# Hybrid megakernel, attention scores: minus the row maximum written into the score banks by ACT and DVE, in place of a fourth matmul

## What is computed

```python
latent_kv = x @ w_kv_down                      # (2, 2048, 128)
k, v = split(latent_kv @ w_kv_up)              # 16 heads of 64
q = (x @ w_q)                                  # 16 heads of 64
att = einsum('bqhd,bkhd->bhqk', q, k) * 64 ** -0.5
att = where(causal, att, -inf)
att = softmax(att, axis=-1)
y = einsum('bhqk,bkhd->bqhd', att, v)
x = x + y.reshape(B, T, 1024) @ w_out
```

## Time and profile before

| | us |
|---|---|
| median of 3 runs | 2118.15 (2118.07 to 2118.34) |
| span of the profiled execution | 2113.7 |
| the rest, outside the span | 4.45 |
| PE busy | 1984.7 (94%) |
| POOL busy | 1425.9 (67%) |
| DVE busy | 1337.2 (63%) |
| ACT busy | 1097.9 (52%) |

### The profile page before, as it was taken

One profiled execution on the slowest core, in us unless ns is written; L12 is line 12 of the kernel. 1 busy time (PEld: TensorE's weight loads), 2 busy tenths in 40 slices (PEclk: granted clock), 3 DMA queues, 4 the chain that ended last, 5 costly groups with the idle time before them and its releaser, 6 DMA issues.

```text
span 2113.7 us, 35206 instructions
## 1 busy us (share of the span) xinstructions
PE 1984.7 (94%) x12886; PEld 1240.9 (59%) x12886; DVE 1337.2 (63%) x2728; ACT 1097.9 (52%) x2236; POOL 1425.9 (67%) x812
## 2 busy tenths in 40 slices
PE   8997788999999999999989999999999999999898
PEld 6775454555655555555555655555555555555466
DVE  7786555576656666666665657576756575656443
ACT  5775543455545454545455444545445445444585
POOL 1333225778687878787857687868786878687822
PEclk9998899999999999999999999999999999999999
DMA  3000000000000000000000000000000000000001
GB/s 124 1 1 1 0 7 13 13 19 10 13 18 16 13 19 12 19 10 19 13 12 17 12 20 11 17 12 20 11 18 11 20 11 18 11 14 11 26 26 60
DMA packets 29243, 37.01 MB, mean 18 GB/s; under 512 B 6928, under 2 KB 20368, under 8 KB 29072
## 3 DMA queue, kind: packets, MB, share of 16 engines
q1 hardware_dynamic: 29072, 34.76, 5.4%
HBM read 30.02 MB, written 4.46 MB: 16 GB/s over the span
## 4 chain that ended last, share of the span: by engine, by line
PE 63%; DVE 14%; POOL 12%; ACT 6%; issue 4%; DMA 1%; POOLq 0%; ACTq 0%; SPq 0%; DVEq 0%
PE heads_out L918 16%; POOL acc L1416 10%; PE beside L723 9%; PE scores L723 7%; PE two_heads L874 7%; PE scores L897 4%; PE scores L903 4%; PE scores L899 4%; PE scores L901 4%; DVE part_max L1112 3%; ACT prob L1331 2%; PE two_heads L723 2%; PE beside L929 2%; PE heads_out L723 1%; DVE wQK_lo L1073 1%
## 5 line engine op out<-in xcount | busy, mean ns | idle before, releaser
L1416 POOL TENSOR_TENSOR acc<-acc,prob 128x1024 f32<-128x1024 f32 (+3 forms) x512 | 1017.9, 1988 | 195.4 <-ACT prob L1331 140.1
L1331 ACT ACTIVATE prob<-scores 128x512 f32<-128x512 f32 (+3 forms) x1280 | 579.4, 539 | 649.2 <-PE scores L903 289.0
L1112 DVE TENSOR_REDUCE part_max<-two_heads 128x2 f32<-128x1024 f32 x384 | 469.3, 1222 | 280.5 <-PE two_heads L874 279.7
L918 PE MATMUL heads_out<-prob,V 128*64 128x512 f32 (+3 forms) x2560 | 544.4, 547 | 0.0
L1109 DVE CUSTOM_DVE_ANT_0 two_heads<-two_heads,mask 128x128 f32<-128x128 f32 (+3 forms) x512 | 242.0, 514 | 180.4 <-PE two_heads L874 180.4
L874 PE MATMUL two_heads<-k_hi,q_hi 64*128 64x512 f32 (+3 forms) x1280 | 274.1, 424 | 62.8 <-DVE part_max L1112 30.6
L918 PEld LDWEIGHTS heads_out<-prob,V 128*64 128x64 f32 x2560 | 156.7, 137 | 232.4 <-issue 209.6
L874 PEld LDWEIGHTS two_heads<-k_hi,q_hi 64*128 64x128 f32 x1280 | 120.6, 184 | 256.6 <-issue 133.4
L897 PE MATMUL scores<-q_hi,k_hi 64*128 64x512 f32 (+3 forms) x1280 | 236.1, 364 | 0.8 <-DVE k_lo L1100 0.5
L903 PE MATMUL scores<-neg_max,sel 64*128 64x512 f32 (+3 forms) x1280 | 235.6, 362 | 0.0
L901 PE MATMUL scores<-q_lo,k_hi 64*128 64x512 f32 (+3 forms) x1280 | 235.5, 362 | 0.0
(11 more groups left out here) (301 smaller groups left out, 2898.7 us busy)
## 6 DMA issues: line engine op xcount, KB each, us to landing
rden<-rden_rows SPq DMA_DIRECT2D x128, 128.0 KB, 2.9
X<-u SPq DMA_DIRECT2D x8, 512.0 KB, 8.7
out<-X SPq DMA_DIRECT2D x8, 512.0 KB, 2.9
wQK_raw<-wQuery SPq DMA_DIRECT2D x16, 192.0 KB, 3.1
wO_raw<-wOut SPq DMA_DIRECT2D x16, 128.0 KB, 2.8
wV_raw<-wValue SPq DMA_DIRECT2D x8, 128.0 KB, 2.9
den<-den_rows SPq DMA_DIRECT2D x64, 4.0 KB
rden_rows<-den SPq DMA_DIRECT2D x64, 4.0 KB, 1.3
```

The source lines that it names most:

```text
L918: made = pe.matmul(heads_out[head(h), x0:], V[vn % NVS][:, tt, p % 2, head(h)], prob[step % NPROB][:, h, x0:], start=t == 0, stop=t == TPB ...
L1112: made = ve.reduce_max(part_max[:, t, :, c:c + 1], two_heads[:, :, 0:width], AX.X)
L1331: ac.activation(prob[step % NPROB][:, h, x0:], bank(task, h)[:, x0:], ACT.Exp).then_inc(empty(task, h)[0], 1)
L1416: po.tensor_tensor(total[:, :, x0:], total[:, :, x0:], new[:, :, x0:], ALU.add).then_inc(acc_ok, 1)
```

## The change

- The fourth pass L903, the tiles `sel` and `neg_max`, the transposes L882 and the copies L1316 are gone.
- `row_max`, 128 queries by 8 values, goes to a DRAM row `top_rows` (1024 fp32, heads first) by a DMA of single elements from SP, and comes back from there in one DMA, broadcast to all 128 partitions, into `top` (128 x 2 x 512 fp32, 512 KB; two buffers). The task is called `spread_max`.
- A new task `seed` stands in the list for each step, one iteration ahead of its scores. ACT writes -`top` into the score banks (576 instructions: 384 of 1024 columns for both heads together, and 64 each of 768, 512 and 256 columns in the diagonal steps). On the 128 columns of the diagonal, DVE writes min(-`top`, `limit`) instead (256 instructions of 128 x 256, the `scalar_tensor_tensor` below); `limit` is +3e38 where the key is allowed and -3e38 where it isn't.
- The three passes start with `start=False` and accumulate on the seed. The mask of L1122 after the scores is gone, and ACT takes the exponential of both heads in one instruction (640 in place of 1280).
- Where the bank last held another kind of product, PE first runs two plain matmuls over it (`opened`), which happens at the start of the attention only.

```diff
@@ Plan.attention
+            if self.layers_done:
+                for step in steps[s + 2:s + 4]:
+                    self.need("seed", *step)
+            while spreads and spreads[0][0] <= s and self.unseeded(spreads[0][1] - NMAX):
+                self.need("spread_max", spreads.pop(0)[1])
             for idx, t in steps[max(0, s - 2):s]:
                 self.need("weigh", idx, t)
                 self.need("accumulate", idx, t)
@@ tensor_program, score
-                    for h in range(2):
-                        pe.matmul(bank(task, h)[:, x0:], sel[head(h), :], neg_max[idx % NMAX][head(h), x0:], start=False, stop=True).then_inc(full(task, h)[0], 1)
+                    if c == j:
+                        w.wait_ge(seeded_masked, plan.seeds[idx, t][0]["DVE"])
+                    else:
+                        w.wait_ge(seeded, plan.seeds[idx, t][0]["ACT"])
...
+                    for n, (k, q) in enumerate(terms((k_hi[g], k_lo[g]), (q_hi[i], q_lo[i]))):
+                        for h in range(2):
+                            made = pe.matmul(scores[:, first + h, x0:], k[head(h), kc], q[head(h), x0:], start=False, stop=n == 2, skip_group_check=True)
+                    made.then_inc(full(task)[0], 1)
@@ vector_program
-                        for h in range(2):
-                            w.wait_ge(*full(task, h))
-                        ve.tensor_tensor(scores[:, first:first + 2, x0:x0 + P], scores[:, first:first + 2, x0:x0 + P],
-                                         limit[:, :].unsqueeze(1).broadcast_to([P, 2, P]), ALU.min).then_inc(masked, 1)
+                        w.wait_ge(*top_here(idx))
+                        if x0 < BLK - P:
+                            w.wait_ge(seeded, plan.seeds[idx, t][0]["ACT"])
...
+                        ve.scalar_tensor_tensor(out=scores[:, first:first + 2, x0:x0 + P], in0=top[idx % NMAX][:, :, x0:x0 + P], scalar=-1.0,
+                                                in1=limit[:, :].unsqueeze(1).broadcast_to([P, 2, P]), op0=ALU.mult, op1=ALU.min).then_inc(seeded_masked, 1)
@@ scalar_program
+                        ac.activation(scores[:, first:first + 2, x0:], top[idx % NMAX][:, :, x0:], ACT.Copy, scale=-1.0).then_inc(seeded, 1)
...
-                    for h in range(2):
-                        w.wait_ge(*full(task, h))
-                        ac.activation(prob[step % NPROB][:, h, x0:], bank(task, h)[:, x0:], ACT.Exp).then_inc(empty(task, h)[0], 1)
+                    w.wait_ge(*full(task))
+                    ac.activation(prob[step % NPROB][:, :, x0:], scores[:, first:first + 2, x0:], ACT.Exp).then_inc(empty(task)[0], 1)
@@ sync_program
+                elif kind == "minus_max":
+                    idx = task[1]
+                    w.wait_ge(row_max_ok, idx + 1)
...
+                    sp.dma_start(top_rows[idx % NTOP, :].rearrange("(a p) -> p a", p=P), row_max[:, idx % 2, :, :].rearrange("p h t -> p (h t)"), allow_slow_non_contiguous=True).then_inc(top_out[idx % 2], 16)
+                elif kind == "spread_max":
+                    idx = task[1]
+                    w.wait_ge(top_out[idx % 2], 16 * (idx // 2 + 1))
...
+                    sp.dma_start(top[idx % NMAX].rearrange("p h x -> p (h x)"), top_rows[idx % NTOP:idx % NTOP + 1, :].broadcast_to([P, 2 * BLK])).then_inc(top_in[idx % 2], 16)
```

202 lines of the change are left out of this document (113 added, 89 removed).

## The result

The changed kernel takes 2451.85 us (2445.93 to 2463.09, 4 runs), the kernel before 2118.24 in the same session: a ratio of 1.1581 (95% interval 1.155 to 1.1612), 334 us slower. Slower was forecast, but by 3%; the time lies 167 us above the upper end of the range.

What follows compares the result with a forecast made beforehand. PE was taken as the main bound, with 63% of the last-ending chain plus 4% issue. 2113.7 - 112 + 177 = 2179 us of span, plus 4.45 outside it, gave 2183 us, slower by 3%; range 2025 to 2285 us.

Steps and rivals of the forecast that it cites:

- -112 + 177: Whole span: PE's saved passes and transposes, then DVE's held seeds, work queued behind them and bank 0, both at 67%.
- PE's gain: On PE: 129 us from passes and 38 from transposes, 167 less in all, counted as -112 us.
- the factor: On PE's savings and new delays: 67%, PE's share of the last-ending chain with issue, taken to move the end.
- 32 us of bank 0: Full iterations whose filler used bank 0: ACT's seed waits 0.4 us in each of some 80.
- the walk: One iteration followed from its first score pass: ACT's full-step seed hidden by PE's fillers and `weigh`, unless bank 0 was used.
- the place: Where full steps end and a diagonal begins: PE took 6.47 us for the iteration, with two fillers.
- My own ring: ACT in a full iteration: exponentials end by 3.05 us, first seed at 4.1 plus 0.6 for each filler ahead.
- 168 + 64 us: Diagonal iterations: 128 holds of DVE's second seed at 1.3 us, plus 0.5 us each for the reduction queued behind.
- the first seed's hold: DVE's first seed of a diagonal pair, held by POOL: taken as hidden by PE's own work.
- with the holds at half price: The forecast's own lower bound, with holds of DVE's seeds costing half: 2115 us.
- ten iterations ahead: Row maxima were said to lie some ten iterations ahead of their use, so scatter and broadcast count as hidden.
- Rival C: Units with j = 1 start some 7 us late, as scatter and broadcast take 16 us: 2295 us, chance 0.06.

Runs made afterwards that it cites:

- e4: The kernel before without the fourth pass L903, the making of neg_max kept, maximum not subtracted: 2059.5 us.
- e7: e3 with ACT's seeds cut to 64 columns a head, PE's first pass beginning the sum anew: 2076.8 us.
- e3: The changed kernel with both contiguous rows to DRAM and DVE taking the minimum in the bank: 2219.5 us.
- e2: The changed kernel with the scatter written as 128 contiguous rows of 32 bytes instead of single elements: 2404.6 us.
- e11: e2 with POOL's accumulates (t > 1) cut to 64 columns a head, DVE's seed unchanged: 2184.0 us.
- e10: e7 with DVE's seed from two SBUF tiles put back in place of the minimum in the bank: 2275.2 us.
- e1: The changed kernel with ACT seeding all columns and DVE taking the minimum in the bank, single-element scatter kept: 2376.7 us.
- e13: e3 with constant seeds and no broadcast, but the single-element scatter, SP's wait for it and a small read to a spare tile: 2252.6 us.
- e9: The kernel before with both heads' exponentials merged into one instruction: 2110.5 us, ratio 0.9989.

## Why the prediction was wrong, step by step

From before to the changed kernel one path leads through the runs (ratio differences, in us): pass gone, -55 (e4); all the rest of the change with short ACT seeds and contiguous rows, the transposes gone too, +19 (e7); full length of ACT's seeds, +141 (e3); the hold, +185 (e2); single elements, +44 (the changed kernel). The sum is +334, as it must be for differences of neighbours. On another path the last two are 157 and 72.

The forecast was -112 + 177 = +65, so 269 us are missing. Along this path they are 76 on PE's gain (-36 measured for the first two parts, in place of -112), 120 on ACT's seeds (141 in place of 21), 30 on the hold (185 in place of 155) and 44 on the DMAs (in place of nothing).

**PE's loss: direction right, size too large.** Forecast -112 for passes and transposes, of which 86 are the passes; e4 shows 55 for these, with an interval of 16. The failed step is the factor: 67%, PE's share of the chain with the issue time, was applied to all of it, and it was 0.43 (0.3 to 0.55). With 129 us gone, PE waited longer for the reductions and ACT for the mask (above). PE still has 62% of e4's chain, so the share doesn't tell this; why the factor is lower was not tried further. The transposes, 25 us of the forecast, were not tried alone. PE's busy time, which was to fall by 160 us, rose by 62.

**ACT's seeds: the largest miss.** Forecast: hidden, but for 32 us of bank 0, 21 after the factor; measured: 141 for their length alone. The price of one was right, 1.04 against 1.02 us measured. (ScalarE: Activation LUTs in the Trainium skill, section What ACT_TABLE_LOAD costs, gives 1039 ns by its formula; the trace agrees, with 1020 for the median.) What failed was the walk: it was made at one place, where PE took 6.47 us for an iteration. 320 iterations between 290 and 2030 us take 5.4 us in the mean, and 5.0 with the two passes of 0.23 gone; the place had more of PE's work than most. My own ring had the first seed at 4.1 us plus 0.6 for each filler, the second one 1 us later. At 5.0 us there is no cover for two of them. That this is what failed is argued from the ring; what e7 shows is the price of the length. I also wrote nothing for what stands behind the seeds on ACT: `oT_hi`, for which POOL waited 291.3 us in the changed kernel, 207.2 in e3, 116.5 in e7, 107.1 before.

**DVE's seed: mechanism right, size near, in part by luck.** Forecast 168 + 64 us, times 0.67: 155. Measured 185 and 199 without the scatter, 72 beside it. That POOL's instruction holds it is shown (e11), and the ends 0.29 and 0.30 us behind POOL's ends are those of the earlier trace rows (0.28). (SBUF — State Buffer in the Trainium skill, section Who interferes with whom, has the rule of the shared ports; e2 and e11 agree: a median of 1105 ns with POOL in long instructions, 434 with short ones.) In e2 the seeds are 256 x (1291 - 434) = 219 us longer than unheld ones and in e10, with a mean of 1271, 214: of these 185 and 199 us moved the end, a factor of 0.84 and 0.93 in place of 0.67. A held seed stops PE in its next instruction. In the forecast the first seed's hold was hidden, though its own walk had that seed end at 1118.28, 0.94 us after PE wanted it; the pair at 1206.06, of which PE waited for both (0.75 and 0.46 us), shows that it isn't. So the hold itself and the factor were too low, and the 64 us for what is queued behind, which no run measured, made up for a part. The bound of 2115 us "with the holds at half price" doesn't come out of the terms either: they give 2127 us with the 168 halved, 2105 with the 64 as well.

**DMAs: counted as hidden, wrong.** Measured: 44 us beside the hold, 157 without it. I took 7.4 us as the bound for the scatter; it was 9.7. (DMA: Bandwidth & Descriptors in the Trainium skill, section Rules for kernel authors, gives a descriptor for each element; the packets agree, 57344 more than with contiguous rows, and those rows land in 2.3 us.) But the miss was not the 2.3 us. Two steps failed. One was to price the scatter by when its own data are needed: that doesn't help `rden`, which stands behind it in SP's list. I had written down that the `rden` chain is queued behind, and gave it no number. The other was that the maxima lie ten iterations ahead. That is so for j = 0; with j = 3 the first seed comes 14.6 us after the scatter in the changed kernel (median) and 9.0 in e1, some two iterations. Rival C had the late spread, at 6%, at the units with j = 1, where no seed waited for `top` in e1 or in the changed kernel. Its 112 us (16 units, 7 us each) lie near the 115 that e1, e3 and e13 leave for a late `top`, because there are 16 units with j = 3 too, which waited 7.5 us each in e1; as to the place that is luck.

**Mask behind the scores, merged exponentials.** Counted as nothing; e9 shows 2 us for the exponentials. The mask alone was not tried.

**Clock: not in the sum.** e7, e3, e10 and the changed kernel have the same 11358 matmuls, and PE is busy for 1878.4, 1927.7, 1989.9 and 2046.9 us. Two stretches of the changed kernel (length, PE, PEld, DVE, ACT, POOL, clock):
```profile
1175.00:1200.00 25.00, 22.52 (x143) 11.97 (x139) 13.51 (x28) 19.35 (x25) 19.88 (x10) 1.00 0.15 38
...
1225.00:1250.00 25.00, 19.13 (x102) 10.11 (x103) 13.77 (x23) 16.48 (x27) 11.23 (x7) 0.80 0.12 33
```
Where PE was busy for 22.52 of 25 us it had the full clock of 2.4 GHz; in the second it was busy for 19.13, with waits, and part of the time it had the lower level, 1.2 GHz, which makes 0.80 in the mean. Over the whole span the lower level was granted for 412 us in the changed kernel, 103 in e7 and 86 in the kernel before. So waits for seeds and DMAs are in part paid a second time by slower matmuls. The four kernels bound this: of the 169 us of busy time between e7 and the changed kernel 122 are matmuls with the next one right behind them, and 47 are those with a wait behind them, which there show their full length. How much of it moved the end was not separated from the waits, and stays open.

What the forecast got right: the direction, that held seeds are the largest single term in it, the place where PE waits for them, and what ACT has to do (seeds of 508 us forecast and 489.2 measured; 1570 and 1487.9 in all, of which 34.5 are the merged exponentials with their 544.9 for 579.4). None of the experiments beats the kernel before by anything but leaving work out; e9, at -0.11%, is the only complete one at its level. e7 bounds the idea: with seeds that cost ACT almost nothing, no hold and no scatter, it stands 35 us under the kernel before, and the real length of ACT's seeds is worth 141.

## What to carry to other kernels

Where an in-order queue issues a transfer, price it by what stands behind it in that queue, not only by when its own data are needed; 1024 single elements held up what stood behind them by some 10 us. And look for the unit whose data are ready last, here the one with the most keys. Before new work on an engine is called hidden, compare the whole ring of waits with the mean time of an iteration, not with one place. An engine's share of the chain is a rough price in both directions: here 129 us taken from PE moved the end by 0.43 of them, at a share of 67%, and some 215 us of new stalls right before PE's matmuls by 0.84 to 0.93. When two causes overlap, remove both and each alone: here the same edit showed 72 or 185 us.
